# The normalised rows for tokens without an expert, made tile by tile on ScalarE instead of in one GpSimd operation per group

## What is computed

```python
x = layernorm(x + attention(x, bv_q, bv_k, bv_v))
x = layernorm(x + ffn(x, w_router, w_gate, w_up, w_down))

# attention: Q = sign(x * sign(bv_q)), K = sign(x * sign(bv_k)), V = x * sign(bv_v)
attn = where(causal, sigmoid(4 * Q K^T / 16), 0);  out = attn V
# ffn: 32 experts, each token goes to its first choice; an expert takes its first 320 tokens
out = where(accepted, expert(x)[slot] * gate, 0)
```

## Time and profile before

| what | value |
|---|---|
| time, three runs | 684.07, 687.56, 689.95 us; median 687.56 |
| profiled execution | span of 678.2 us; the page gives no other time for it, and the median lies 9.4 us above this span |
| TensorE | busy 604.2 us (89%), mean granted clock 0.965 |
| VectorE | busy 485.0 us (72%) |
| ScalarE | busy 353.4 us (52%) |
| GpSimd | busy 415.3 us (61%) |
| chain that ended last | PE 68%, DVE 9%, issue 8%, ACT 6%, POOL 5%, DMA 2% |
| 100 to 310 us (two of the four batches), PE busy | 178.1 of 200 us from 110 to 310 us |

### The profile page before, as it was taken

One profiled execution on the slowest core, in us unless ns is written; L12 is line 12 of the kernel. 1 busy time (PEld: TensorE's weight loads), 2 busy tenths in 40 slices (PEclk: granted clock), 3 DMA queues, 4 the chain that ended last, 5 costly groups with the idle time before them and its releaser, 6 DMA issues.

```text
span 678.2 us, 14737 instructions
## 1 busy us (share of the span) xinstructions
PE 604.2 (89%) x4175; PEld 504.3 (74%) x4214; DVE 485.0 (72%) x1300; ACT 353.4 (52%) x678; POOL 415.3 (61%) x547
## 2 busy tenths in 40 slices
PE   5989898899879898988999879999999999999960
PEld 4878787698768687876888637877788778878750
DVE  2669978879787989698898624666776677766740
ACT  5566566456455655666555312555445554555520
POOL 4563757467857377765576520566666666676773
PEclk9999999999999899899999998999999999999995
DMA  8962021132201112206111020566555565566300
GB/s 273 368 211 78 32 80 59 37 96 94 94 29 62 50 39 93 86 23 219 58 59 49 31 87 28 148 193 187 169 158 176 171 190 168 159 184 195 118 32 21
DMA packets 68206, 78.11 MB, mean 115 GB/s; under 512 B 7934, under 2 KB 59374, under 8 KB 68160
## 3 DMA queue, kind: packets, MB, share of 16 engines
q1 hardware_dynamic: 60992, 63.26, 30.1%
q0 software_dynamic: 7168, 14.30, 5.9%
HBM read 44.29 MB, written 37.90 MB: 121 GB/s over the span
## 4 chain that ended last, share of the span: by engine, by line
PE 68%; DVE 9%; issue 8%; ACT 6%; POOL 5%; DMA 2%; SPq 0%; ACTq 0%; DVEq 0%; POOLq 0%
PE ps L877 13%; PE ps L738 8%; PE ps L739 6%; PE ps L740 6%; PE ps L862 6%; PE ps L864 5%; PE ps L863 5%; PE ps L716 5%; PE ps L846 5%; PE ps L765 4%; DVE hl_ring L929 4%; DVE xrow L957 2%; PE ps L757 2%; ACT hl_ring L574 2%; POOL out_dram L490 2%
## 5 line engine op out<-in xcount | busy, mean ns | idle before, releaser
L738 PE MATMUL ps<-v_hl,hl_ring 128*128 128x256 f32 x544 | 176.6, 325 | 25.6 <-DVE hl_ring L929 16.7
L739 PE MATMUL ps<-v_hl,hl_ring 128*128 128x256 f32 x544 | 156.0, 287 | 0.0
L740 PE MATMUL ps<-v_hl,hl_ring 128*128 128x256 f32 x544 | 155.6, 286 | 0.0
L738 PEld LDWEIGHTS ps<-v_hl,hl_ring 128*128 128x128 f32 x544 | 105.9, 195 | 51.5 <-issue 28.4
L490 POOL DMA_INDIRECT out_dram<-alone,ids x96 | 108.0, 1125 | 55.8 <-ACT alone L665 22.5
L572 ACT ACTIVATE a_ring<-ps 128x512 f32<-128x512 f32 (+3 forms) x160 | 85.7, 535 | 91.1 <-PE ps L716 49.9
L929 DVE TENSOR_TENSOR hl_ring<-a_ring,hl_ring 128x512 fp32r<-128x512 f32 (+3 forms) x160 | 119.1, 748 | 19.0 <-ACT hl_ring L574 8.8
L409 POOL DMA_INDIRECT expert_rows<-xrow,slot x64 | 68.7, 1074 | 63.9 <-issue 26.1
L739 PEld LDWEIGHTS ps<-v_hl,hl_ring 128*128 128x128 f32 x544 | 106.2, 195 | 1.9
L740 PEld LDWEIGHTS ps<-v_hl,hl_ring 128*128 128x128 f32 x544 | 106.0, 195 | 0.0
L877 PE MATMUL ps<-xall,a_ring 128*128 128x256 f32 (+1 forms) x384 | 95.9, 392 | 1.1 <-DVE a_ring L1107 1.1
(11 more groups left out here) (108 smaller groups left out, 1125.3 us busy)
## 6 DMA issues: line engine op xcount, KB each, us to landing
expert_rows<-xs SPq DMA_DIRECT2D x40, 258.0 KB, 5.6
xs<-expert_rows SPq DMA_DIRECT2D x32, 258.0 KB, 3.0
xall<-in_L_attn_x_dram SPq DMA_DIRECT2D x16, 512.0 KB, 4.1
out_dram<-alone SPq DMA_DIRECT2D x16, 512.0 KB, 3.1
xall<-in_L_ffn_w_gate_dram SPq DMA_DIRECT2D x32, 256.0 KB, 3.6
xall<-in_L_ffn_w_up_dram SPq DMA_DIRECT2D x32, 256.0 KB, 3.9
xall<-in_L_ffn_w_down_dram SPq DMA_DIRECT2D x32, 256.0 KB, 4.2
xs<-expert_rows SPq DMA_DIRECT2D x32, 64.5 KB, 3.0
```

What stands on the lines that cost most here:

```text
L738: mm(o, ah, v_hl[:, 0, j, :], start=(j == 0), stop=False)
L739: mm(o, ah, v_hl[:, 1, j, :], start=False, stop=False)
L740: last = mm(o, al, v_hl[:, 0, j, :], start=False, stop=(j == GT * g + i))
```

## The change

ScalarE makes the alone rows, one 128x256 tile per activation with the scale as an operand of one value per partition, instead of GpSimd's one product per group. A new table ALONE gives the step of each of a group's four tiles: for group 3 steps 7, 8, 10 and 10 of the next batch, for the others of its own batch. In a step they stand behind the two sigmoids, the copy of x and the gate's sigmoids, and ahead of `keys`, `signs` and `values_high` (L555). The semaphore alone_ready now counts tiles, so its waits are multiplied by four: those of SyncE's stores and that of GpSimd's `rstd`. What is left of GpSimd's `rows_alone` is called `rows_numbered` and waits for the scatter two groups back. The last group's rows are made after the last `gates`.

```diff
+ALONE = {3: (7, 8, 10, 10), 0: (16, 17, 18, 19), 1: (24, 25, 26, 27), 2: (32, 34, 36, 38)}
...
             def store_alone(G, par):
-                atleast(sp, alone_ready, G + 1)
+                atleast(sp, alone_ready, (G + 1) * GT)
...
             def rstd(G, par):
                 atleast(pool, mv_ready, (G + 1) * GT, settle=True)
-                atleast(pool, alone_ready, G, settle=True)
+                atleast(pool, alone_ready, G * GT, settle=True)
...
-            def rows_alone(G, half, par):
-                atleast(pool, rstd_step, G * RN + RN, settle=True)
-                atleast(pool, x1_ready, (G + 1) * GT, settle=True)
-                atleast(pool, alone_out[par], half * 16, settle=True)
-                g_.tensor_tensor(alone[:, par, :, :], xrow[:, par, :, 0:D],
-                                 small[:, 5, :].unsqueeze(2).broadcast_to([P, GT, D]), ALU.mult)\
-                    .then_inc(alone_ready, 1)
+            def rows_numbered(G, half, par):
+                atleast(pool, scattered[par], half * 16 * GT, settle=True)
                 g_.tensor_copy(xrow[:, par, :, D + 1].bitcast(U32), tok[:, :]).then_inc(tok_step, 1)
...
+            def rows_alone(G, half, par, tiles=range(GT)):
+                act.wait_ge(rstd_step, (G + 1) * RN)
+                act.wait_ge(x1_ready, (G + 1) * GT)
+                atleast(act, alone_out[par], half * 16)
+                for i in tiles:
+                    s_.activation(alone[:, par, i, :], xrow[:, par, i, 0:D], ACT.Copy,
+                                  scale=small[:, 5, i:i + 1]).then_inc(alone_ready, 1)
...
                         if k == EXPS[g]:
                             gates(bb * NG + g)
+                        for i in range(GT):
+                            if k == ALONE[g][i]:
+                                rows_alone(bb * NG + g, 2 * b + {3: -1, 0: 0, 1: 0, 2: 1}[g], g % 2, range(i, i + 1))
...
             gates(B * NG - 1)
+            rows_alone(B * NG - 1, 2 * B - 1, 1)
```

More of the change, by code:

```diff
@@ L242, in bass_postln_attn_moe_kernel @@
         block = ctx.enter_context(nc.Block())
+        RN = 6
         M0, M1 = 6, 7
@@ L365, in values_low @@
                     .then_inc(v_ready, 1)
-            RN = 6
             def rstd(G, par):
                 atleast(pool, mv_ready, (G + 1) * GT, settle=True)
-                atleast(pool, alone_ready, G, settle=True)
+                atleast(pool, alone_ready, G * GT, settle=True)
                 base = G * RN
@@ L417, in batch @@
                     rstd(n - 1, 1)
-                    rows_alone(n - 1, 2 * b - 1, 1)
+                    rows_numbered(n - 1, 2 * b - 1, 1)
                 rstd(n, 0)
@@ L421, in batch @@
                 values_low(b, 2)
-                rows_alone(n, 2 * b, 0)
+                rows_numbered(n, 2 * b, 0)
                 if not first:
@@ L428, in batch @@
                     pool.wait_ge(zero_out, 16 * (SLOTS // (P * ZR)))
-                rows_alone(n + 1, 2 * b, 1)
+                rows_numbered(n + 1, 2 * b, 1)
                 scatter(n, 0)
@@ L434, in batch @@
                     values_signed(b + 1, 0)
-                rows_alone(n + 2, 2 * b + 1, 0)
+                rows_numbered(n + 2, 2 * b + 1, 0)
                 scatter(n + 1, 1)
@@ L495, in _ @@
             rstd(last + 3, 1)
-            rows_alone(last + 3, 2 * B - 1, 1)
+            rows_numbered(last + 3, 2 * B - 1, 1)
             scatter(last + 3, 1)
```

## The result

| | before | changed |
|---|---|---|
| median of the timed runs, us | 688.75 (4 runs, 684.07 to 693.3) | 703.08 (4 runs, 701.62 to 707.85) |
| ratio, with its 95% interval | | 1.0223 (1.0162 to 1.0285) |
| span of the profiled execution, us | 678.2 | 701.6 |
| TensorE busy; mean granted clock | 604.2 us (89%); 0.965 | 612.4 us (87%); 0.946 |
| VectorE, ScalarE, GpSimd busy, us | 485.0, 353.4, 415.3 | 466.8, 376.3, 371.6 |

The change makes the kernel 2.2% slower, some 14 us. The forecast was 706 us in a range of 697 to 716. Runs that are more than 1.5% above the fastest of their kernel count as slow and are left out of the ratios, which are not exactly the quotients of the medians beside them. ScalarE has 23 us more to do and GpSimd 44 us less, and neither number is near the 14 us.

What follows compares the result with a forecast made beforehand. The bound was who waits for whom in attention's ScalarE-VectorE-TensorE chain at steps 11 and 12. Terms 18.4 (hold) + 1.7 (clock) - 1.9 (L395) + 0.6 (`rstd`) = 18.8 us, on 687.6: 706 us, range 697 to 716.

Steps and rivals of the forecast that it cites:

- The hold: Step 10, batches 1 to 3: ScalarE waits at V's high part for GpSimd; net 6.7, 6.7 and 5.0 us.
- rival 1: Step 10: the wait is covered by early tiles or sigmoids, leaving only small terms; 686 us, chance 0.06.
- What was given back: Batches 1 and 2, step 9: shorter L974 returns 0.9 us each; batch 3: L929 no longer held returns 2.1.
- The clock: After TensorE's stop at step 10: low clock adds 1.7 us in batch 3, nothing more in batches 1 and 2.
- The activation's length: Each 128x256 tile on ScalarE: 0.50 us long, 0.45 us apart.
- 64 activations at nothing: ScalarE outside step 10: 29 us of added activations cost nothing, covered by slack against VectorE and TensorE.
- `rstd` of group 1: GpSimd waits for ScalarE's step 19: 0.6 us (0 to 2) in batch 0, nothing in batches 1 to 3.
- L395 off GpSimd: Steps 23 and 31, five places where L395 held VectorE and TensorE then idled: 1.9 us less.
- rival 2: VectorE set free: all 15.0 us of operations held beside L395 come back; 672.6 us, chance 0.04.
- the turn of the loop: SyncE's stores and loads of x move later, including a load after step 38: put at nothing.
- The base: Median of the runs stands 9.4 us above the span of before; kept on top of the forecast span of 697.0 us.

Runs made afterwards that it cites:

- Experiment 2: Changed kernel with group 3's four tiles in steps 7, 7, 8 and 8 instead of 7, 8, 10 and 10: 685.95 us, ratio 0.9968.
- Experiment 3: Changed kernel with a second buffer for the alone rows' scales, so `rstd` waits for the group two back; tiles left in place: 688.69 us, ratio 0.9988.
- experiment 4: Changed kernel with V's high part for quarter 2 in step 14 instead of 10: 674.29 us, ratio 0.9785.
- Experiment 10: Changed kernel with V's high part at step 14, group 2's last tiles at step 35 and every alone-row activation made twice: 687.53 us, against 673.18 without doubling.
- experiment 8: Kernel before with GpSimd's product for the alone rows (L395) cut to one column of 256: 684.94 us, ratio 0.9941.
- the second pair: One more profile each of the kernel before and the changed kernel, both unedited: spans 686.0 and 703.0 us.
- experiment 1: Changed kernel run again without edit, with more rounds: 705.63 us, ratio 1.0243 to the kernel before.
- experiment 6: Kernel before with V's high part for quarter 2 in step 14 instead of 10: 681.97 us, ratio 0.9899.

## Why the prediction came out right, and what was wrong in it

**The hold: right in mechanism, place and size.** The sum named the wait at V's high part, 6.7 + 6.7 + 5.0 us net. Both pairs of profiles have 6.6 + 6.6 + 4.9. Experiments 2 and 3 each remove it and land at -0.3% and -0.1%, where rival 1 had put the covered wait (686 us); experiment 4 shows that it is ScalarE's standing and not GpSimd's lateness. In detail GpSimd, in batch 2, ran from L378 to the end of L359 in 5.98 us, not 6.49: VectorE was idle beside it.

**What was given back: right.** L981 (L974 before) takes 0.29 us where V's product no longer runs beside it, against 1.18 in the earlier trace rows. In batch 3 it is 1.6 us in place of 2.1.

**The clock: its effect right, its length not.** The prediction said it would be wrong in size if the low clock lasted much longer than 3.4 us, and it lasted 10.2 us and more. Batch 3 paid 1.4 and 1.7 us in the two pairs, 1.7 predicted. Batches 1 and 2, at nothing in the sum, have -0.4 and 0.2 us in the first pair and 2.4 and 0.5 in the second, so there the low clock's price is not separated from the spread. That it stays small is because TensorE has room, as I read it: it is busy for 6.57 of the 10.2 us in batch 2's window above, and VectorE for 8.62.

**The activation's length: right.** 0.50 us each was taken between two rows; 64 of them measure 492 to 598 ns with a middle of 512. The formula of the Trainium skill, page "ScalarE: Activation LUTs", section "What ACT_TABLE_LOAD costs", had given an estimate of 0.49 us, and the shortest measured is 492 ns.

**64 activations at nothing: no price seen for the first set, refuted for a second.** The prediction says "Outside step 10 they cost nothing", from the slack of single steps, each looked at alone. Experiment 10 prices a second set at 13 to 14 us, over half of the busy time that it adds, so the slack was there once and not twice. The first set shows no price of its own in the profiles. Its one candidate is step 30: in batch 3 it takes 2.78 us before and 3.58 to 3.62 us in every kernel with one set, but already 3.37 us in experiment 8, which has no activation there, only L395 gone. That leaves 0.2 us.

**`rstd` of group 1: right in batch 0, missed in the others.** Step 22 of batch 0 takes 0.70 us more, 0.6 predicted. Batches 1 to 3 were put at nothing, since `rstd` would be late "by some 1 us and the layer norm at step 21 has room". It is 1.0 us late in batch 3 and there is no room: 0.46 to 0.52 us more in the first pair of profiles, 1.5 us together. Experiment 3, which takes this wait away, has step 22 at 2.02 or 2.03 us in all four batches.

**L395 off GpSimd: 1.9 us, measured 4.1** (1.6 to 6.6) in experiment 8. The interval reaches down to my value. The first two profiles show 3.1 us at the five places alone, the second pair 1.8: I had counted TensorE's idle time there and not how late the held operation came. The Trainium skill, page "SBUF — State Buffer", section "SBUF: two separate sides", describes the shared port as an exclusive lock between VectorE and GpSimd; the lock is in the trace (L1023 up to 1342 ns beside L395, L1024 at most 173 without it), but rival 2, which made a gain of all of it, is refuted by the same run.

**Missed: the turn of the loop.** The prediction moved SyncE's transfers and costed them at nothing, on their own deadlines. It did not ask what else uses the DMA engines when they run. With group 2's last tile at step 38, 1.05 MB go out and in just as VectorE enters the loop's next turn. Step 0 of batch 2 then takes 8.2 us in all six profiles, against 4.83 and 7.35 us in the two of the kernel before, so it cost 3.4 us in the one pair and 0.9 in the other.

**The base.** I took the 9.4 us between the span of 678.2 us and the median as work around the execution. The profiled execution of the changed kernel has a span of 701.6 us and a time of 703.44: 1.8 us lie around it. The profile of before was simply a short execution; the second one has 686.0 us. The argument needed only differences, so the sum kept its meaning. But against the medians the change costs 14.3 us (703.08 - 688.75), or 15.5 us in experiment 1's runs (16.8 by the ratio), and 17.0 us between the spans of the second pair, while the sum said 18.8. That 706 came within 3 us of the measured time is therefore in part luck: the span was forecast 4.6 us too short (697.0 against 701.6), and the 9.4 us put on top of it are 1.8. In the sum, too, terms that were missed on either side (step 22 and the loop's turn against step 35 and more at steps 23 and 31) stand against each other.

**Where the balance does not close.** With V's high part at step 14 the rows on ScalarE are 7.7 us better than on GpSimd (experiments 4 and 6; 7.9 by the ratios). The terms measured here are -4.1 (L395), +2.2 (step 22) and +0.9 to 3.4 (step 0 of batch 2), together -1.0 to +1.5. So some 7 us of gain or more have no name there. With the wait covered the gap is smaller: experiments 2 and 3 lie 4.2 and 1.5 us below the kernel before, 2.2 and 0.8 by the ratios, within the spread of what these terms give. One candidate is the VectorE subtractions that a GpSimd product holds: by my count, over the free lengths, 25.9 us in the profile of experiment 6, and 13.1 in that of experiment 4. Experiment 8 has 24.7 us of these holds and is still below the kernel before. This stays open.

## What to carry to other kernels

When a wait is moved to another engine, write down what stands behind it on both engines. Here the tiles and their only consumer's consumer stood in one in-order queue, with another engine between them, and two tiles of 0.91 us together became a stop of 6.4 us; that one sum predicted the result. Then ask whether the thing waited for has to stand there at all: moving V's high part by four steps gave the changed kernel 31 us, twice what the change had cost, and the kernel before 8 us. A low busy share of an engine does not make more work on it free without end where it sits between the links of the critical chain: one set of activations fitted, the second did not. One profile is one execution: two profiles of one kernel differed by 3.4 us at one step here, so a term is to be sought in a second pair before it is believed. The transfers that a reorder shifts must be checked against what else happens at that moment.

## What the runs showed of the hardware that I had not expected

- At the turn of the loop (step 0 of batch 2) VectorE stops for 5.04 to 5.56 us, idle time put down to "issue", in the six profiles in which a store and a load of 512 KB each start just ahead of it, and for 2.35 to 2.75 us in the eight others. In the changed kernel 1.55 MB move in the 9 us from 205 us, 1.05 of them this store and load; before, 0.47 MB in as long a window. The window of each of the two kernels has two packets of the DMA queue for instructions. That these packets stand behind the transfers is a guess; no run took the store and the load apart.
- A stop of 6.2 us was followed by 10.2 to 13.7 us at the 1.2 GHz level, counted from where the clock fell, one of 1.58 us by 3.4 us.
- A GpSimd product can hold even a 128x4 operation of VectorE for 1.2 us, and a VectorE block can lengthen a GpSimd product: V's product takes 2.90 us beside four L964 in experiment 4, and 2.34 beside an idle VectorE.
